# Ranking the experts two token tiles at a time with scalar compares, and idle products of TensorE at five seams

## The reference, cut to what matters

```
x = LN(x + self_attention_16_heads(x))          # layer 0
x = LN(x + cross_attention_8_heads(x, ctx))
x = LN(x + ternary_ffn(x))                      # Hadamard, 8-bit activations, ternary weights
x = LN(x + attention_32_heads_8_kv(x))          # layer 1, window 128, sinks
x = LN(x + experts_by_token_id(x))              # 4 experts, chosen by the token's id
logits = x @ gate_w.T                           # [1024, 32]
scores = sigmoid(logits); sel = top_k(scores, 4)
w = softmax(logits)[sel] / sum                  # weight of each of the 4 choices
x = LN(x + sum_k w_k * (expert[sel_k](x) + 0.05 * small_expert[sel_k // 2](x)))
```

## Time and profile before

| | |
|---|---|
| time, median of 3 runs | 869.49 us (867.83 to 869.85) |
| the profiled execution's own time | 866.02 us |
| its span | 864.2 us |
| mean granted clock of TensorE | 0.926 of full speed |
| TensorE matmul (PE) busy | 755.0 us, 87% of the span |
| VectorE (DVE) busy | 611.7 us, 71% |
| ScalarE (ACT) busy | 456.0 us, 53% |
| GpSimd (POOL) busy | 432.3 us, 50% |

### The profile page before, as it was taken

One profiled execution on the slowest core, in us unless ns is written; L12 is line 12 of the kernel. 1 busy time (PEld: TensorE's weight loads), 2 busy tenths in 40 slices (PEclk: granted clock), 3 DMA queues, 4 the chain that ended last, 5 costly groups with the idle time before them and its releaser, 6 DMA issues. The chain is left out here.

```text
span 864.2 us, 18065 instructions
## 1 busy us (share of the span) xinstructions
PE 755.0 (87%) x5738; PEld 471.7 (55%) x5738; DVE 611.7 (71%) x2052; ACT 456.0 (53%) x1447; POOL 432.3 (50%) x428
## 2 busy tenths in 40 slices
PE   6899889887949999999999999998755499999944
PEld 3566666665824444555555555787545355555523
DVE  1646777797766777888888888342345768888856
ACT  2367877674431000888888888100333077777724
POOL 4345655562004665766666666000630478888840
PEclk9959999999969999999999999999785589999977
DMA  9400000000003666300000000250368222222225
GB/s 325 182 2 2 2 1 2 2 2 1 1 13 89 169 171 157 98 2 1 2 2 1 2 2 1 110 207 25 120 231 210 99 67 74 74 80 73 73 63 190
DMA packets 32237, 63.17 MB, mean 73 GB/s; under 512 B 6592, under 2 KB 21068, under 8 KB 31280
## 3 DMA queue, kind: packets, MB, share of 16 engines
q1 hardware_dynamic: 20704, 41.40, 14.9%
q0 software_dynamic: 4896, 11.95, 4.4%
q10 hardware_dynamic: 6544, 8.67, 3.8%
HBM read 41.01 MB, written 9.84 MB: 59 GB/s over the span
## 5 line engine op out<-in xcount | busy, mean ns | idle before, releaser
L1405 ACT ACTIVATE a_room<-a_room,a_nm 128x257 f32<-128x257 f32 x256 | 127.3, 499 | 100.6 <-DVE a_nm L1248 99.8
L1447 POOL TENSOR_TENSOR a_room<-a_room,a_rd 128x1024 f32<-128x1024 f32 x64 | 121.3, 1895 | 65.8 <-DVE a_rd L1256 65.4
L1248 DVE CUSTOM_DVE_ANT_0 a_room<-a_ps,table,NSK 128x256 f32<-128x256 f32 x256 | 107.8, 477 | 0.4 <-PE a_ps L1107 0.4
L823 ACT ACTIVATE l_Pr<-l_Sm,l_nm 128x128 f32<-128x128 f32 (+1 forms) x192 | 88.3, 461 | 37.0 <-DVE l_nm L643 22.9
L909 POOL TENSOR_TENSOR l_Pr<-l_Pr,l_rd 128x256 f32<-128x256 f32 (+1 forms) x80 | 82.0, 1043 | 50.5 <-DVE l_rd L657 50.3
L1107 PEld LDWEIGHTS a_ps<-room 64*128 64x128 f32 x512 | 44.1, 186 | 53.2 <-issue 48.5
L1107 PE MATMUL a_ps<-room 64*128 64x256 f32 x512 | 72.3, 402 | 0.5 <-DVE a_nm L1248 0.5
L1187 PE MATMUL a_ps<-a_room,W 128*128 128x512 f32 x160 | 71.5, 605 | 0.8 <-ACT a_room L1419 0.8
L1228 DVE SCALAR_TENSOR_TENSOR a_room<-a_ps,BQK,table 128x512 f32<-128x512 f32 x80 | 56.3, 746 | 21.9 <-PE a_ps L1187 20.1
L1122 PE MATMUL a_ps<-table,a_room 128*128 128x128 f32 x512 | 69.7, 279 | 1.1 <-ACT a_room L1414 1.1
L1135 PE MATMUL a_psO<-a_room,room 128*64 128x512 f32 x256 | 68.8, 617 | 0.0
(11 more groups left out here) (313 smaller groups left out, 1756.6 us busy)
## 6 DMA issues: line engine op xcount, KB each, us to landing
room<-a_room SPq DMA_DIRECT2D x96, 64.0 KB, 2.1
room<-a_room ACTq DMA_DIRECT2D x96, 64.0 KB, 2.1
room<-in_w_in SPq DMA_DIRECT2D x1, 6144.0 KB, 17.3
room<-in_c_in SPq DMA_DIRECT2D x1, 4096.0 KB, 13.1
room<-pairs SPq DMA_DIRECT2D x8, 512.0 KB, 7.7
W<-in_w SPq DMA_DIRECT2D x1, 3072.0 KB, 13.0
room<-in_w_out SPq DMA_DIRECT2D x1, 3072.0 KB, 20.2
W<-in_wo SPq DMA_DIRECT2D x1, 2048.0 KB, 8.3
```

Of the source, the lines that this page charges most:

```text
L823: nc.scalar.activation(Pr[:, t % 4, n, 0:n_keys], Sm[:, t % 2, n, 0:n_keys], ACT.Exp, bias=nm[:, t % 2, n:n + 1], scale=-1.0, accum_out=de ...
L1248: nc.vector.tensor_tensor_reduce(out=Sm[:, t % 2, n, 0:S], in0=psS(t)[:, n // 2, n % 2, :], in1=c["window"][:, n % 2, :], scale=-1.0, scal ...
L1405: nc.scalar.activation(Pr[:, t % 4, n, :], Sm[:, t % 2, n, :], ACT.Exp, bias=nm[:, t % 2, n:n + 1], scale=-1.0, accum_out=den[:, t % 2, n: ...
L1447: pool.tensor_tensor(p, p, rd[:, t % 2, :].unsqueeze(2).to_broadcast([P, 4, S]), ALU.mult).then_inc(normed, 1)
```

## The change

1. A helper `spin` issues `count` products of the identity with a 128 x 256 table (fp32), into a bank of PSUM that nobody reads. It is called in `project_0` (5 before the last `turn`, behind a wait on `v_kept`, and 3 after it), in `layer_0` (3 behind `score(0)`, 3 each in steps 0 and 1, 8 at the very end), in `token_experts` (6 before the loop, 16 behind it) and in `experts` (5 at the start).
2. In `token_experts` the logits of each pair g go to a bank of their own; ScalarE makes `exp(-logit)` and the copy per pair, between its `keep_z`; VectorE does the sigmoid, the eight largest and their places per pair, still in this block. `route` begins with the conversion of the places.
3. In `route` the sum over the four choices is two additions in place of the reduction and the cast. `in_tile` (compare and multiply in one) and `in_place` are written by one `tensor_scalar` for each of the 32 pairs, whose position and number are [128, 1] operands; GpSimd has nothing to do there.

```diff
@@ -39,6 +39,12 @@
+def spin(nc, c, out, count):
+    for _ in range(count):
+        nc.tensor.matmul(out[:, 0:S], c["ident"], c["causal"], start=True, stop=True, skip_group_check=True)
@@ -231,7 +237,10 @@
                     turn(t - 1)
+            pe.wait_ge(v_kept, NT - 1)
+            spin(nc, c, psV[:, 0], 5)
             turn(NT - 1)
+            spin(nc, c, psV[:, 0], 3)
@@ -585,9 +594,12 @@
             score(0)
+            spin(nc, c, psO[:, 1], 3)
             for t in range(steps):
...
                     score(t + 1)
+                if t < 2:
+                    spin(nc, c, psO[:, 1], 3)
                 if 0 <= t - LT < slots:
@@ -625,6 +637,7 @@
                 down(2 * p + 1)
+            spin(nc, c, psT[:, 0], 8)
@@ -1500,7 +1513,10 @@
         s = {n: st.sem("te_" + n) for n in ("xT", "xt", "h", "sg", "a", "aT", "at", "down", "taken", "stat", "mixed",
-                                           "std", "rstd", "normed", "zT", "zt", "logits")}
+                                           "std", "rstd", "normed", "zT", "zt", "logits", "exp", "rank")}
+        def logits_of(g):
+            return (psL[:, 0:2 * NE], psH[:, 0, 0:2 * NE], psH[:, 1, 0:2 * NE], psY[:, 0, 0:2 * NE])[g]
         block = stack.enter_context(nc.Block())
@@ -1568,7 +1584,9 @@
+            spin(nc, c, psL, 6)
             staggered([x_turn, up, a_turn, down], NSORT)
+            spin(nc, c, psL, 16)
@@ -1583,9 +1601,13 @@
                     pe.wait_ge(loads["gate"], 16)
+                if g == 1:
+                    pe.wait_ge(s["a"], NSORT)
+                if g == 3:
+                    pe.wait_ge(s["taken"], NSORT)
                 for t in range(2):
                     for kk in range(KD):
-                        last = nc.tensor.matmul(psL[:, (2 * g + t) * NE:(2 * g + t + 1) * NE], zT[:, g % 2, t, kk, :],
+                        last = nc.tensor.matmul(logits_of(g)[:, t * NE:(t + 1) * NE], zT[:, g % 2, t, kk, :],
                                                 GW[:, kk, :], start=(kk == 0), stop=(kk == KD - 1))
@@ -1622,6 +1644,13 @@
+            def keep_logits(g):
+                act.wait_ge(s["logits"], g + 1)
+                pair = slice(2 * g, 2 * g + 2)
+                raw = logits_of(g).rearrange("p (t e) -> p t e", t=2)
+                nc.scalar.activation(tiles.sc[:, pair, :], raw, ACT.Exp, scale=-1.0).then_inc(s["exp"], 1)
+                nc.scalar.activation(tiles.lg[:, pair, :], raw, ACT.Copy)
@@ -1637,12 +1666,11 @@
             keep_z(2)
+            keep_logits(0)
             keep_z(3)
-            act.wait_ge(s["logits"], G)
-            nc.scalar.activation(tiles.sc[:, :, :], psL[:, 0:NT * NE].rearrange("p (t e) -> p t e", t=NT),
-                                 ACT.Exp, scale=-1.0)
-            nc.scalar.activation(tiles.lg[:, :, :], psL[:, 0:NT * NE].rearrange("p (t e) -> p t e", t=NT),
-                                 ACT.Copy)
+            keep_logits(1)
+            keep_logits(2)
+            keep_logits(3)
@@ -1671,6 +1699,18 @@
                                             ALU.subtract, ALU.mult).then_inc(s["normed"], 1)
+            link = Chain(dve, s["rank"]).link
+            sc = tiles.sc
+            for g in range(G):
+                pair = slice(2 * g, 2 * g + 2)
+                dve.wait_ge(s["exp"], g + 1)
+                link(nc.vector.tensor_scalar(sc[:, pair, :], sc[:, pair, :], 1.0, None, ALU.add))
+                link(nc.vector.reciprocal(sc[:, pair, :], sc[:, pair, :]))
+                for t in range(2 * g, 2 * g + 2):
+                    last = nc.vector.max(tiles.top[:, t, :], sc[:, t, :])
+                link(last)
+                for t in range(2 * g, 2 * g + 2):
+                    nc.vector.max_index(tiles.idx[:, t, :], tiles.top[:, t, :], sc[:, t, :])
@@ -1687,9 +1727,7 @@
         nmx = st.sb("ro_nmx", [P, NT])
-        picks = st.sb("ro_picks", [P, NT, NE])
-        top = st.sb("ro_top", [P, NT, 8])
-        idx = st.sb("ro_idx", [P, NT, 8], U32)
+        picks = st.sb("ro_picks", [P, 2, NT, NE])
         idf = st.sb("ro_idf", [P, NT, 8])
@@ -1713,7 +1751,7 @@
         s = {n: st.sem("ro_" + n) for n in (
-            "shift", "dve", "bf16", "chosen", "ranked", "located", "numbered", "owned", "rowed", "placed",
+            "shift", "dve", "bf16", "chosen", "ranked", "numbered", "owned", "rowed", "placed",
             "ordered")}
@@ -1758,35 +1796,18 @@
-        @block.gpsimd
-        def _(pool):
-            for k in range(TOPK):
-                which = slice(k * NT, (k + 1) * NT)
-                pool.wait_ge(s["located"], k + 1)
-                pool.tensor_tensor(in_tile[:, which, :], in_tile[:, which, :].bitcast(F32),
-                                   c["pairs"][:, which].unsqueeze(2).to_broadcast([P, NT, NTILE]),
-                                   ALU.mult).then_inc(s["numbered"], 1)
...
-            link(nc.vector.tensor_scalar(sc[:, :, :], sc[:, :, :], 1.0, None, ALU.add))
-            link(nc.vector.reciprocal(sc[:, :, :], sc[:, :, :]))
-            for t in range(NT):
-                last = nc.vector.max(top[:, t, :], sc[:, t, :])
-            link(last)
-            for t in range(NT):
-                last = nc.vector.max_index(idx[:, t, :], top[:, t, :], sc[:, t, :])
-            link(last)
-            link(nc.vector.tensor_copy(idf[:, :, :], idx[:, :, :]))
+            link(nc.vector.tensor_copy(idf[:, :, :], tiles.idx[:, :, :]))
             link(nc.vector.tensor_tensor(
...
                 ALU.is_equal))
-            link(nc.vector.tensor_reduce(picks[:, :, :], sel.rearrange("p k t e -> p t e k"), AX.X, ALU.add))
-            nc.vector.tensor_copy(chosen[:, :, :], picks[:, :, :]).then_inc(s["chosen"], 1)
+            link(nc.vector.tensor_tensor(picks[:, :, :, :], sel[:, 0:2], sel[:, 2:4], ALU.add))
+            nc.vector.tensor_tensor(chosen[:, :, :], picks[:, 0], picks[:, 1], ALU.add).then_inc(s["chosen"], 1)
@@ -1823,12 +1844,14 @@
             for k in range(TOPK):
-                which = slice(k * NT, (k + 1) * NT)
-                for out, width, of, done in ((in_tile, NTILE, tile, "located"), (in_place, P, place, "placed")):
-                    nc.vector.tensor_tensor(out[:, which, :],
-                                            c["slots"][:, 0:width].unsqueeze(1).to_broadcast([P, NT, width]),
-                                            of[:, which].unsqueeze(2).to_broadcast([P, NT, width]),
-                                            ALU.is_equal).then_inc(s[done], 1)
+                for i in range(k * NT, (k + 1) * NT):
+                    last = nc.vector.tensor_scalar(in_tile[:, i, :], c["slots"][:, 0:NTILE], tile[:, i:i + 1],
+                                                   c["pairs"][:, i:i + 1], ALU.is_equal, ALU.mult)
+                last.then_inc(s["numbered"], 1)
+                for i in range(k * NT, (k + 1) * NT):
+                    last = nc.vector.tensor_scalar(in_place[:, i, :], c["slots"][:, 0:P], place[:, i:i + 1], None,
+                                                   ALU.is_equal)
+                last.then_inc(s["placed"], 1)
@@ -1889,6 +1912,8 @@
         self.total = st.sb("ti_total", [P, NT])
+        self.top = st.sb("ti_top", [P, NT, 8])
+        self.idx = st.sb("ti_idx", [P, NT, 8], U32)
@@ -2000,6 +2025,7 @@
             held, owners = {}, {}
+            spin(nc, c, psD[:, 1], 5)
             for k in range(NTILE + 3):
```

## The result

Five runs of each kernel on one chip gave 861.79 us median (859.82 to 862.00) against 867.83 us (864.21 to 869.85): a ratio of 0.9949, 95% interval 0.9929 to 0.9969. By the ratio the change makes the kernel about 4.4 us faster (2.7 to 6.2; the two medians alone lie 6.0 apart), where 11.9 us were forecast. The time itself lies inside the stated range of 852 to 864 us, 4.2 us above the forecast of 857.6 us, which rests on the 869.49 us of the three runs known then. The profiled execution has a span of 860.1 us, 4.1 less than before. TensorE's mean granted clock is 0.951, before 0.926.

The account below looks back on a forecast made before the run. It took TensorE's half-clock stretches after idle gaps and a VectorE chain from logits to `experts` as bounds. 3.4 - 0.5 + 1.0 + 5.0 + 1.1 + 0.9 + 1.0 = 11.9 us off the median gave 857.6 us, range 852 to 864.

Parts of the forecast that it names:

- The two tables: `route`: VectorE alone writes `in_tile` and `in_place`, TensorE paces the rounds; 9.4 us against 10.4, of which 0.9 won counted.
- Rival B: `route`: the 64 short table instructions don't overlap; 6.2 us lost in place of 0.9 won, 864.7 us; chance 0.08.
- Seam 4: Logits and ranking: sixteen products give full clock, ranking goes by pairs; 5.0 us won, 3.3 with the clock at half.
- Seam 2: End of `layer_0`: eight idle products delay the block, the clock may rise; 0.5 us lost (4.3 lost to 2.1 won).
- Seam 1: `project_0` to `layer_0`: idle products keep the clock whole into `layer_0`, five slots run at full clock; 3.4 us won.
- Rival A: `project_0` to `layer_0`: clock may fall in the first slots; 3.4 us gone, nine products cost 2; 863.0 us; chance 0.15.
- Seam 3: Start of `token_experts`: six products raise the clock sooner, three tiles save 2.5 us, less 1.5 delay; 1.0 us won.
- the sum over choices: `route`: two additions replace the reduction and most of a cast; 1.1 us won, all on the chain.
- seam 5: Start of `experts`: five products end 0.7 us late but the clock rises some 3 us sooner; 1.0 us won.
- C: All idle products: they don't raise or hold the clock and run at 0.9 us; 16.1 us slower, 885.6 us; chance 0.05.
- D: Whole kernel: the clock is not what holds it; only the choice of experts counts, 5.3 us; 864.2 us; chance 0.06.

Follow-up runs that it names:

- The probes: Kernel after with 60 more `tensor_scalar` at the end of `route`, by width and operand kind, results unused; one execution: 0.089 to 0.211 us apart at 40 elements.
- held clock: Kernel after with nineteen products ahead of the logits' transposes, four between, long VectorE tables, no products ending `layer_0`: ratio 0.9893 to the kernel before.
- third group: Last experiments, on one chip beside the kernel before (880.15 us): kernel after again (0.9961), two long-table kernels (0.9893 each), one adding idle products in `route` (0.9894).

## Why the prediction was off

**The two tables (forecast +0.9, measured -4.8): the step that failed.** The term that failed is VectorE's price of a short `tensor_scalar`. The prediction took the five of the earlier trace rows, 0.323 us apart, for one element per cycle and 0.056 us fixed, and priced everything else from that: 0.098 us for `in_tile`, 0.123 for `in_place`, 1.8 us for each k, so that TensorE would pace the rounds. They take 0.211 and 0.195 us, 3.25 us for each k, and TensorE waits for VectorE. The probes show that the same 0.323 us is 0.52 ns an element (two per cycle, by the cycle of the prediction's own 256 / 0.96), 0.07 fixed and twice 0.06 for the two [128, 1] operands. At 256 elements the two readings give the same number; at 40 elements they give 0.098 and 0.211. The one row that could tell them apart was quoted, the instruction with constants at 0.29 us, 0.12 less than L2218. It was used for the width of `in_place` but not for the price of the operand. The Trainium skill ("VectorE: DVE Perf Modes", The perf-mode tier table) gives fp32 `tensor_scalar` from SBUF two elements per cycle; the prediction said that the trace disagreed, and it was wrong in that: L1880 and L1884 both grow by 0.52 ns an element, as does L1886.

**Rival B** had the right sign and almost the right size (6.2 lost) for the wrong reason. The instructions do overlap: each of L1878 lasts 294 ns, and they start 211 ns apart. What the row of short ones pays is the operands. The Trainium skill (same page, The TRN2 errata) gives about 150 cycles as the fixed term of one instruction, and the prediction's estimate charged it to each start: 0.20 us at 40 elements and 0.29 at 128. The trace agrees only at 40 elements with two [128, 1] operands (0.211); with constants the same instruction is 0.089 us behind the one before it, and 128 elements with one operand are 0.195. That 4.8 came near 6.2 is luck.

**Seam 4 (5.0, measured 3.3): the clock term.** The prediction gave 3.3 us for the case that the clock stays at half, and chose the other. In the trace the clock fell at 646.8, 3.2 us behind the end of the products and 1.9 us into the transposes and logits. The runs without products (3.1) and with a held clock (15.96 - 11.58 = 4.4) give both cases: the ranking by pairs is worth 3.1 and the whole clock 1.3. So about 1.1 of the missing 1.7 us is the fall, and the rest is that both parts were put slightly too high (3.3 and 1.7). The end of the sixteen products ahead of the norm (643.56 against 644.92) was right.

**Seam 2 (-0.5, measured -1.9).** That the block would end late and the clock fall again behind the barrier was in the text as one of the ends; the delay, 1.5 us at the barrier, lies within its 0.7 to 4.3. What was over-priced is the return: the clock rose under the products and fell again at 254.3, so of 2.8 us nothing came back. The -1.9 is that of one pair of traces; over all kernels the eight products cost about 1 us at the gather, and without them the ratio is not told from that of the kernel after.

**Seam 1 (3.4, measured 3.8).** The mechanism is as forecast: clock 1.00 throughout, slots 2.43 us apart from the fourth on. Five slots gave 15.83 - 12.07 = 3.8 us and not 3.4, as they took 2.41 each and not 2.48, and that is all of it. The third reciprocal stands 12.32 us behind the last `turn` (51.50 - 39.18), where it stood 12.29 before (52.06 - 39.77): the nine products took back what the first slots gained, as was assumed. The seam alone gave the same 3.8 us. Rival A is out.

**Seam 3 (1.0, measured 0.8), the sum over choices (1.1 and 1.1), seam 5 (1.0 and 1.2)** were right in mechanism and size. At seam 3 the six products put the first transposes off by 1.8 us (from the gather's issue to them it took 3.11 us before, 4.94 here), as allowed for.

**Rivals C and D.** C is out: the products hold the clock at seam 1 and are followed by a rise at seams 2, 3 and 5. D gave 5.3 us for a kernel in which the clock counts for nothing; the total came close to it (4.4) by accident. The kernel without products is not faster than before at all, since there the 3.1 + 1.1 us of the ranking and the sum are taken back by the tables.

## What to carry to other kernels

Before you price a short instruction from a long one, split the long one with a second row that has another width or another kind of operand; one row has two unknowns, and here the wrong split cost a factor of two at 40 elements. Prefer one broadcast `tensor_tensor` over many `tensor_scalar` with [128, 1] operands: comparing and multiplying 320 elements took 2 x 0.49 us in two long ones, 8 x 0.21 = 1.7 us in eight short ones, and comparing 1024 took 1.22 us in one, 8 x 0.195 = 1.6 us in eight. Idle products paid where they fill a gap that ends in a long stretch of TensorE work (3.8 us for seventeen products); where the barrier of seam 2 followed, the clock fell again and about 1 us of delay stayed, and behind the sixteen products ahead of the logits it fell in six of seven traces, and there nothing was gained.

## What the runs showed of the hardware

- A `tensor_scalar` of VectorE in a row costs 0.07 us, 0.52 ns per fp32 element, and 0.06 us for each [128, 1] operand; a constant is free.
- A 320-element comparison on VectorE took 0.49 us with GpSimd idle, and 1.00 us where it started while GpSimd multiplied the table before it. The second ended 0.35 us behind GpSimd's product (678.47 against 678.12). The 1024-element comparison, already running when that product began, took 1.22 us, the same as without GpSimd. So not every instruction beside GpSimd slows; why this one does, no run shows. Timeline of the kernel before:

```profile
676.32 1.22 DVE L1828 TENSOR_TENSOR ro_in_place<-table,ro_place 128x1024 fp32r<-128x1024 f32 x1
676.49 1.63 POOL L1766 TENSOR_TENSOR ro_in_tile<-ro_in_tile,table 128x320 fp32r<-128x320 f32 x1 [33.59 <-DVE ro_in_tile L1828]
677.46 1.01 DVE L1828 TENSOR_TENSOR ro_in_tile<-table,ro_tile 128x320 fp32r<-128x320 f32 x1
```

- The kernel before took 1.2 to 1.4% longer on the three chips of the experiments than in the first comparison, and there waits are put down to "remote", of which the traces of before and after in the first comparison have none. `experts`, from its first transposes to those of its sums, took 153.9 and 152.7 us in the first comparison and 159.6 to 163.8 on the three chips. The waits of the kernel after in the third group, `token_experts` and `experts` (us in total, times, longest):

```profile
ACT ex_sg L2130 <- remote: 12.8, 9, 1.8
DVE te_y L1685 <- remote: 3.4, 1, 3.4
```

What they wait for no run shows. They come in every kernel of the three groups, and their number in `experts` differs (two to nine, 2.2 to 13.3 us). It does not follow the length alone: the kernel with the old tables (159.6 us) has two and the three longest (163.6 to 163.8 us, all on the third chip) have nine, but the kernel without products (162.7 us) has two as well.
